# Distance attention of a decoder: both query halves in one group of products, value products between the groups

## The chip, the cores and the metric

The kernel runs on one core of a Trainium2 chip. The metric is the device time of one execution in microseconds (us), here the median of three runs.

## The reference, cut to what matters

The kernel is a two-layer decoder on x of 1024 tokens by 128 features. Six blocks follow one another, each with a residual sum and a layer norm. The change touches only the first, an attention whose weights come from distances, with 16 heads of width 64:

```python
P = X @ W_in + b_in                       # per head Q, K, V, G, 64 wide each
d2 = q2[..., :, None] + k2[..., None, :] - 2.0 * qk
cdist = jnp.sqrt(jnp.maximum(d2, 0.0))
W = jnp.power(EPS + cdist, -2)
W = W / (EPS + jnp.sum(W, axis=-1, keepdims=True))
A = jnp.einsum('hbts,hbse->hbte', W, V)
H = (G * A).transpose(1, 2, 0, 3).reshape(b, t, HEADS * 64)
return H @ W_out + b_out
```

q2 and k2 are the squared norms of the queries and of the keys. All of it is float32. The five blocks behind it (a gated network over a context of 6404 rows, two mixtures of experts, a rotary attention, a cross attention and a last attention) are the same in both kernels.

## The kernel before, in words

The stage is `distance_attention`. The order of work on each engine is written out by hand, and the engines meet in semaphores. The heads are taken as 8 pairs; the two heads of a pair stand in partitions 0 to 63 and 64 to 127. The stage goes through bodies b = 0 to 8 and a closing part. Body b makes the distances of pair b and, from b = 2 on, does the value products, sums and output of pair b - 2.

A body on TensorE, in this order: the projections to queries and keys (`project_qk`, line 193); from body 3 on the output projection of pair b - 3 (line 304); value products of key chunks 0 and 1 of pair b - 2 (line 240); the norms of the queries and of the keys (lines 201 and 206); the sums of the weights (line 250); value products of chunks 2 and 3; the projections to values and gates (lines 213 and 218); then for each of 8 chunks of 128 keys and each half of 512 queries the distances. One distance group is two products K*Q, one for each head, contracting 64 rows (line 224), and behind them two products that add the query norms, contracting 3 rows in bf16 (line 229: the norm is split in three bf16 parts that add up). In the chunks 0 to 3 the value products of chunks 4 to 7 stand ahead of the two groups.

PSUM (`PS`) has eight banks. Banks 0 to 3 are two slots of two banks each: everything that VectorE reads takes the slots in turn. `TURN` numbers what is made, `room` makes TensorE wait until VectorE has taken what stood in the slot before (`s_taken`), and `s_made` tells VectorE that a slot is full. Banks 4 and 5 add up the value products, banks 6 and 7 the output.

A body on VectorE: squares of the queries and keys (lines 354 to 362), the split of the query norms (lines 368 to 374, over 64 partitions), a copy of the key norms (line 377), the copy of the sums (line 385), bias on values and gates (lines 393 and 397), then for each chunk and half two instructions that add the key norm and cut at zero, from PSUM to the tile D (line 405), and last the gated product (line 415). ScalarE takes the root of four chunks at a time, then logarithm and exponential (lines 480 to 490). GpSimd adds the weights over chunks (lines 545 and 550).

Of the kernel before, what the change touches and what calls it, by code (L numbers as in the profile page):

```python
# [18 lines left out]
BF16 = mybir.dt.bfloat16  # L19
# [4 lines left out]
P = 128  # L24
T = 1024
HALF = 512
NT = T // P
# [5 lines left out]
PAIRS = HEADS // 2  # L33
D0 = 64
# [49 lines left out]
def half(ap, h):  # L84
    return ap[:, h * HALF:(h + 1) * HALF]


def distance_attention(nc, PS, x, w, Y, onesd, fixed):
# [4 lines left out]
    PIECE = NT // 2  # L93
    BODIES = PAIRS + 2
    LAST = PAIRS - 1

    def turns(b):

        made = ["q", "k", "q2", "k2"] if b < PAIRS else []
        dist = [("d", c, h) for c in range(NT) for h in range(2)] if b < PAIRS else []  # L100
        vg = ["v", "g"] if b < PAIRS else []
        return made + (["sum"] if b >= 2 else []) + (dist + vg if b == 0 else vg + dist)
# [10 lines left out]
    with ExitStack() as ctx:  # L113
        n = Names(nc, ctx, "dist")
# [1 line left out]
        wout = n.sb("wout", [P, PAIRS, P])  # L116
        bias = n.sb("bias", [P, 3, PAIRS])
        bv = n.sb("bv", [P, PAIRS * P])
        selq = n.sb("selq", [P, D0])
        selk = n.sb("selk", [P, 2])  # L120
        rows = n.sb("rows", [P, 2])
        Q = n.sb("Q", [P, T])
# [3 lines left out]
        G = n.sb("G", [P, 3, T])  # L126
        D = n.sb("D", [P, 2, 2, NT, T])
        k2 = n.sb("k2", [P, NT, 2])
        p0 = n.sb("p0", [D0, T], BF16)
        rest = sq[0:D0, 0, :]  # L130
        q2 = n.sb("q2", [D0, T], BF16)
        wsum = n.sb("wsum", [P, 2, T])
        ones = n.sb("ones", [P, D0])
        onesb = n.sb("onesb", [P, P], BF16)
# [28 lines left out]
        with nc.Block() as block:  # L163
# [17 lines left out]
            def _(pe):  # L181
                def room(b, k):

                    if TURN[b, k] >= 2:
                        pe.wait_ge(s_taken, TURN[b, k] - 1)
                    return slot(b, k)
# [7 lines left out]
                                             start=True, stop=True)  # L194
                        last.then_inc(s_made, 1)

                def norms(b):
                    at = room(b, "q2")
                    pe.wait_ge(s_sq, 2 * b + 1)
                    for h in range(2):  # L200
                        last = pe.matmul(PS[0:D0, at + h, :], selq[:, :], half(sq[:, 0, :], h), start=True, stop=True)
                    last.then_inc(s_made, 1)
                    at = room(b, "k2")
                    pe.wait_ge(s_sq, 2 * b + 2)
                    for c in range(NT):
                        last = pe.matmul(PS[:, at, 2 * c:2 * c + 2], sq[:, 1, c * P:(c + 1) * P], selk[:, :],
                                         start=True, stop=True, skip_group_check=True)
                    last.then_inc(s_made, 1)

                def project_vg(b):  # L210
                    at = room(b, "v")
# [6 lines left out]
                        last = pe.matmul(PS[:, at + h, :], wp[:, b % 2, 3 * P:4 * P], half(x, h), start=True, stop=True)  # L218
                    last.then_inc(s_made, 1)

                def distances(b, c, h):
                    at = room(b, ("d", c, h))
                    for s in range(2):
                        pe.matmul(PS[:, at + s, :], K[D0 * s:D0 * s + D0, c * P:(c + 1) * P],  # L224
                                  Q[D0 * s:D0 * s + D0, h * HALF:(h + 1) * HALF], start=True, stop=False)
                    if c == 0 and h == 0:
                        pe.wait_ge(s_q2, b + 1)
                    for s in range(2):
                        last = pe.matmul(PS[:, at + s, :], onesb[32 * s:32 * s + 3, :],  # L229
                                         q2[32 * s:32 * s + 3, h * HALF:(h + 1) * HALF], start=False, stop=True)  # L230
                    last.then_inc(s_made, 1)

                def values(p, c):

# [74 lines left out]
                for b in range(BODIES - 1):  # L309
                    if b < PAIRS:  # L310
                        project_qk(b)
                    if b == 0:
                        pe.wait_ge(s_const, 4 * 16)
                        pe.wait_ge(s_set, 4)
                    if b >= 3:
                        projection(b - 3)
                    if b >= 2:
                        values(b - 2, 0)
                        values(b - 2, 1)
                    if b < PAIRS:  # L320
                        norms(b)
                    if b >= 2:
                        sums(b - 2)
                    if b >= 2:
                        values(b - 2, 2)
                        values(b - 2, 3)
                    if 0 < b < PAIRS:
                        project_vg(b)
                    for c in range(NT):
                        if b >= 2 and c < PIECE:  # L330
                            values(b - 2, PIECE + c)
                        for h in range(2 if b < PAIRS else 0):
                            distances(b, c, h)
                    if b == 0:
                        project_vg(b)
                closing()
# [2 lines left out]
            def _(dve):  # L339
# [7 lines left out]
                def made(b, k):  # L347
                    dve.wait_ge(s_made, TURN[b, k] + 1)
                    return flat(PS[:, slot(b, k):slot(b, k) + 2, :])
# [13 lines left out]
                    dve.wait_ge(s_sq, 2 * b + 2)  # L363
                    dve.sem_inc(s_taken, 1)

                def norms(b):
                    of = made(b, "q2")[0:D0]
                    own.up(dve.tensor_copy(p0[:, :], of))
                    own.done()
                    dve.scalar_tensor_tensor(rest, p0[:, :], rows[0:D0, 0:1], of, ALU.mult, ALU.add).then_inc(s_taken, 1)  # L370
                    dve.wait_ge(s_taken, TURN[b, "q2"] + 1)
                    own.up(dve.tensor_copy(p0[:, :], rest))
                    own.done()
                    dve.scalar_tensor_tensor(q2[:, :], p0[:, :], rows[0:D0, 1:2], rest, ALU.mult, ALU.add
                                             ).then_inc(s_q2, 1)
                    of = made(b, "k2")
                    dve.tensor_copy(flat(k2), of[:, 0:2 * NT]).then_inc(s_taken, 1)
                    dve.wait_ge(s_taken, TURN[b, "k2"] + 1)

                def totals(p):  # L380

# [1990 lines left out]
def _layout(inputs):  # L2372

    f = {k: np.asarray(v) for k, v in inputs.items()}
    W = f["L0_attn_W_in"].reshape(P, PAIRS, 2, 4, D0)
    wpair = np.concatenate([W[:, :, h, i] for i in range(4) for h in range(2)], axis=2).transpose(1, 0, 2)
    b = f["L0_attn_b_in"].reshape(HEADS, 4, D0)
    selq = np.zeros((2, D0, 2, 32), np.float32)
    selk = np.zeros((2, D0, 2), np.float32)
    drows = np.zeros((4, 32, 2), np.float32)  # L2380
    for h in range(2):
        selq[h, :, h, 0:3] = 1.0
        selk[h, :, h] = -0.5
    drows[:, 1:3, 0] = drows[:, 2, 1] = -1.0
    a = {
        "xT": f["x"][0].T,
        "ident": np.eye(P, dtype=np.float32),
        "center": (np.eye(P) - 1.0 / P).astype(np.float32),
        "cols": _columns(f["L0_attn_b_out"], f["L1_xattn_bo"], f["L1_ffn_ln1_w"], f["L1_ffn_ln1_b"],
                         f["L1_ffn_ln2_w"], f["L1_ffn_ln2_b"]),  # L2390
        "wpair": wpair,
        "wout": f["L0_attn_W_out"].reshape(PAIRS, P, P).transpose(1, 0, 2),
        "dbias": b[:, (0, 1, 3)].reshape(PAIRS, 2, 3, D0).transpose(1, 3, 2, 0).reshape(P, 3, PAIRS),
        "selq": selq.reshape(P, D0),
        "selk": selk.reshape(P, 2),
        "drows": drows.reshape(P, 2),
        "bv": np.broadcast_to(b[:, 2].reshape(1, T), (P, T)),
        "ctx": _context(f["ctx_1024"][0]),
        "small0": _small(f["L0_ffn_router_W"], f["L0_ffn_router_b"], f["L0_ffn_b1"], f["L0_ffn_b2"]),
        "experts0": _experts(f["L0_ffn_W1"], f["L0_ffn_W2"]),  # L2400
        "small1": _small(f["L1_ffn_gate_w"], f["L1_ffn_gate_b"]),
        "experts1": _experts(f["L1_ffn_w1"], f["L1_ffn_w2"]),
        **_rotary(f["L1_attn_Wq"], f["L1_attn_Wk"], f["L1_attn_Wv"], f["L1_attn_Wo"]),
        **_aux(),
        **_cross(f["L1_xattn_Wk"], f["L1_xattn_Wv"], f["L1_xattn_Wq"], f["L1_xattn_Wo"]),
        "mask": f["mask_1x1xSxS2_ik1"][0, 0],
        "last_w": f["L1_ffn_w_qkv"],
        "last_wo4": f["L1_ffn_w_proj"].reshape(4, GROUPS, D8, P),
        "last_rows": np.zeros((P, 3, GROUPS), np.float32),
    }  # L2410
    wo4 = np.zeros((4, 32, GROUPS, P), np.float32)
    wo4[:, 0:D8] = a["last_wo4"].transpose(0, 2, 1, 3)
    a["last_wo4"] = wo4.reshape(P, GROUPS * P)
    for j in range(GROUPS):
        a["last_rows"][:, 0, j] = np.arange(P) // D8 % GROUPS == j
        a["last_rows"][:, 1, j] = np.arange(P) % 32 == D8 * ((j + 1) % GROUPS)
        a["last_rows"][:, 2, j] = np.arange(P) % 32 != D8 * ((j + 1) % GROUPS)
    return {k: np.ascontiguousarray(v) for k, v in a.items()}
# [13 lines left out]
```

## Time and profile before

| what | us |
|---|---|
| median of 3 runs | 2407.54 (2407.51 to 2410.68) |
| the profiled execution | 2405.06 |
| its span in the profile | 2403.4 |
| TensorE busy | 2235.0 (93%) |
| ScalarE busy | 1630.8 (68%) |
| VectorE busy | 950.3 (40%) |
| GpSimd busy | 476.3 (20%) |

The span is what the records cover; 1.7 us of the execution lie around it. The busy shares are means over stages with different limits, so they say little on one stage. The stage of the change takes about the first 468 us of the span, the other five blocks the rest.

### The profile page before, as it was taken

Reading aid. Unit: us, or ns where it says so; the run is one execution under the profiler, and the core shown is the slowest. Engines: PE = TensorE matmul, PEld = TensorE weight load, DVE = VectorE, ACT = ScalarE, POOL = GpSimd, SP = SyncE. Lnnn points to the kernel's source line nnn. Section 1 sums busy time; section 2 is a strip of 40 time slices with the busy share of each in tenths; the row PEclk is TensorE's granted clock in tenths of the full one; section 3 lists DMA queues with packets and bytes.
Section 4 is the critical chain, followed back from the end, with each engine's and each line's share of the span. In section 5 each row is a group of like instructions: output and inputs, shape, how many; then the busy total and the mean of one; then the engine's idle time right before and its main releaser. Section 6 shows DMA issues by size and latency. Waiting matters only on the chain. (4 is left out here: it accounts for less than half of the span.)

```text
span 2403.4 us, 30487 instructions
## 1 busy us (share of the span) xinstructions
PE 2235.0 (93%) x12206; PEld 769.8 (32%) x12206; DVE 950.3 (40%) x1489; ACT 1630.8 (68%) x1295; POOL 476.3 (20%) x254
## 2 busy tenths in 40 slices
PE   8999999899979988999899999999999987999898
PEld 3333333344446632222311111111111122222466
DVE  7766676235441156666211111111111115887111
ACT  4998889633333223555599999999999964666533
POOL 0776665200100024666300000000000000000000
PEclk8999999999989998999999999999999996999999
DMA  1000000036644002000100010010000000000010
GB/s 43 9 5 5 5 1 1 27 140 213 208 159 160 26 0 71 1 1 1 23 24 1 1 43 1 1 43 1 1 1 1 1 2 9 1 1 1 21 35 26
DMA packets 29133, 79.00 MB, mean 33 GB/s; under 512 B 3600, under 2 KB 18976, under 8 KB 26928
## 3 DMA queue, kind: packets, MB, share of 16 engines
q1 hardware_dynamic: 15032, 30.71, 4.1%
q0 software_dynamic: 4384, 29.56, 3.5%
q10 hardware_dynamic: 9592, 16.96, 1.9%
q8 instruction: 89, 1.46, 0.2%
q14 instruction: 36, 0.29, 0.0%
HBM read 71.68 MB, written 5.59 MB: 32 GB/s over the span
## 5 line engine op out<-in xcount | busy, mean ns | idle before, releaser
L1889 ACT ACTIVATE crat_E<-banks 128x1536 f32<-128x1536 f32 x536 | 741.7, 1460 | 22.1 <-PE banks L1780 6.8
L1805 PE MATMUL banks<-crat_E,crat_vst 128*32 128x512 f32 (+1 forms) x3264 | 436.3, 607 | 0.5 <-ACT crat_E L1889 0.4
L1780 PE MATMUL banks<-crat_Q,mid_arena 52*128 52x512 bf16 x1600 | 322.7, 385 | 19.5 <-ACT crat_E L1889 15.3
L1916 DVE COPY crat_vst<-all_crossV 128x96 f32<-128x96 f32 x136 | 34.3, 253 | 635.5 <-PE banks L1805 635.4
L550 POOL TENSOR_TENSOR dist_wsum<-dist_wsum,dist_D 128x1024 f32<-128x1024 f32 x88 | 208.1, 2364 | 7.8
L1509 ACT ACTIVATE rotat_E<-banks 128x1024 f32<-128x1024 f32 x128 | 124.0, 1021 | 116.1 <-PE banks L1393 116.0
L405 DVE TENSOR_SCALAR dist_D<-banks,dist_k 128x512 f32<-128x512 f32 x256 | 178.8, 746 | 54.7 <-PE banks L229 53.6
L1780 PEld LDWEIGHTS banks<-crat_Q,mid_arena 52*128 52x128 bf16 x1600 | 59.3, 93 | 435.3 <-ACT crat_E L1889 300.9
L1575 DVE TENSOR_REDUCE rotat_mx<-banks 128x1 f32<-128x512 f32 x256 | 163.5, 685 | 70.0 <-PE banks L1364 68.8
L1509 ACT ACTIVATE lastat_E<-banks 128x1024 f32<-128x1024 f32 x128 | 123.9, 1020 | 85.6 <-PE banks L1385 85.6
L1575 DVE TENSOR_REDUCE lastat_mx<-banks 128x1 f32<-128x512 f32 x256 | 162.4, 685 | 37.8 <-PE banks L1364 35.1
L1521 POOL MEMSET lastat_mb<- 128x2048 f32 x1 | 1.8, 1805 | 802.1 <-POOLq L63 802.1
L1557 POOL TENSOR_TENSOR mid_arena<-rotat_E 128x2048 f32<-128x2048 f32 x31 | 140.4, 4528 | 89.3 <-ACT rotat_E L1509 86.0
L224 PE MATMUL banks<-dist_Q,dist_K 64*128 64x512 f32 x512 | 148.1, 656 | 4.7 <-DVE dist_sq L370 0.5
L843 ACT ACTIVATE mlp_A<-banks 128x1024 f32<-128x1024 f32 x51 | 52.2, 1024 | 136.1 <-PE banks L736 136.1
L940 PEld LDWEIGHTS banks<-moe_W,moe_A 128*128 128x128 f32 x1024 | 122.9, 192 | 45.8 <-issue 26.5
L940 PE MATMUL banks<-moe_W,moe_A 128*128 128x128 f32 x1024 | 125.7, 276 | 11.1 <-DVE moe_acc L1042 11.1
L1805 PEld LDWEIGHTS banks<-crat_E,crat_vst 128*32 128x32 f32 (+1 forms) x3264 | 64.3, 108 | 175.3 <-issue 163.5
L1042 DVE SCALAR_TENSOR_TENSOR moe_acc<-banks,moe_G,moe_acc 128x128 f32<-128x128 f32 x128 | 34.6, 344 | 209.9 <-PE banks L940 209.9
L240 PE MATMUL banks<-dist_D,dist_V 128*64 128x512 f32 x480 | 111.7, 601 | 0.0
L736 PE MATMUL banks<-all_x,mlp_C 128*128 128x512 f32 x204 | 100.2, 616 | 10.1 <-DMA mlp_C<-in_ctx 10.1
L480 ACT ACTIVATE dist_D<-dist_D 128x4096 f32<-128x4096 f32 x24 | 85.5, 3610 | 33.9 <-DVE dist_D L405 33.9
(271 smaller groups left out, 2807.1 us busy)
## 6 DMA issues: line engine op xcount, KB each, us to landing
mlp_M<-in_mask POOLq DMA_DIRECT2D x28, 800.5 KB
mid_arena<-cross_k SPq DMA_DIRECT2D x42, 204.0 KB
moe_W<-in_experts SPq DMA_DIRECT2D x16, 512.0 KB, 3.6
mid_arena<-in_rot_tables ACTq DMA_DIRECT2D x8, 1024.0 KB, 19.2
mlp_C<-in_ctx SPq DMA_DIRECT2D x17, 384.0 KB, 4.5
cross_k<-mlp_kp ACTq DMA_DIRECT2D x17, 288.0 KB, 2.3
mlp_row<-in_mask POOLq DMA_DIRECT2D x1, 3202.0 KB, 12.7
mlp_M<-in_mask POOLq DMA_DIRECT2D x1, 3202.0 KB
```

The lines of the kernel that those rows point to most:

```text
L224: pe.matmul(PS[:, at + s, :], K[D0 * s:D0 * s + D0, c * P:(c + 1) * P], Q[D0 * s:D0 * s + D0, h * HALF:(h + 1) * HALF], start=True, stop=F ...
L240: last = pe.matmul(PS[D0 * s:D0 * s + D0, 4 + h, :], V[:, p % 3, c, D0 * s:D0 * s + D0], D[:, p % 2, s, c, h * HALF:(h + 1) * HALF], start ...
L405: last = dve.tensor_scalar(D[:, b % 2, s, c, h * HALF:(h + 1) * HALF], of[:, s * HALF:(s + 1) * HALF], k2[:, c, s:s + 1], 0.0, ALU.add, AL ...
L550: pool.tensor_tensor(to, to, W[:, c, :], ALU.add).then_inc(s_add, 1)
L736: last = pe.matmul(PS[:, at + h, :], C[:, b, k, 0:P], half(x, h), start=True, stop=True)
L940: last = pe.matmul(PS[:, Y[k] + t // 4, (t % 4) * P:(t % 4 + 1) * P], A[:, f % 2, t * P:(t + 1) * P], W[:, k, FF + f * P:FF + (f + 1) * P] ...
L1509: act.activation(flat(E[:, at % NE, 2 * i:2 * i + 2, :]), flat(PS[:, S + 2 * i:S + 2 * i + 2, :]), ACT.Exp, scale=scale).then_inc(s_e, 1)
L1557: pool.tensor_tensor(flat(ES[:, (4 * ps + k) % 2, :, :]), flat(E[:, at % NE, :, :]), flat(E[:, (at + 1) % NE, :, :]), ALU.add).then_inc(s_ ...
L1575: dve.tensor_reduce(mx[:, t, r, kh:kh + 1], PS[:, MX + i % 2, :], AX.X, ALU.max).then_inc(s_mt, 1)
L1780: last = pe.matmul(PS[:, 3 * (at % 2) + k, :], K[s:s + ROWS, 2 * (g % 2) + pair, c * P:(c + 1) * P], Q[s:s + ROWS, 2 * g + pair, qh * HALF ...
L1805: last = pe.matmul(PS[32 * j:32 * j + 32, 6 + ps % 2, :], vst[keys, (ps * STEPS + c // 3) % 3, c % 3, j, :], E[keys, at // 3 % NE, at % 3, ...
L1889: act.activation(flat(E[:, at % NE, :, :]), flat(PS[:, 3 * (at % 2):3 * (at % 2) + 3, :]), ACT.Exp, scale=CROSS_SCALE).then_inc(s_e, 1)
```

## The change

The two distance groups of a chunk become one: products K*Q of the first query half, then of the second, and behind all four the norm products of both halves. For this both slots have to be free before the group is complete. The query norms are now made in four groups of 32 partitions (so `selq` is 128 wide, and `p0`, `rest` and `q2` have 128 partitions), so that the four norm products contract different row groups. The value products of chunks 2 to 7 stand one behind each of the groups 0 to 5. From body 1 on the key norms are made ahead of the query norms.

```diff
+    def norm_order(b):
+        return ["q2", "k2"] if b == 0 else ["k2", "q2"]
-        made = ["q", "k", "q2", "k2"] if b < PAIRS else []
+        made = ["q", "k"] + norm_order(b) if b < PAIRS else []
-        selq = n.sb("selq", [P, D0])
+        selq = n.sb("selq", [P, P])
-        p0 = n.sb("p0", [D0, T], BF16)
-        rest = sq[0:D0, 0, :]
-        q2 = n.sb("q2", [D0, T], BF16)
+        p0 = n.sb("p0", [P, T], BF16)
+        rest = sq[:, 0, :]
+        q2 = n.sb("q2", [P, T], BF16)
...
-                def distances(b, c, h):
-                    at = room(b, ("d", c, h))
-                    for s in range(2):
-                        pe.matmul(PS[:, at + s, :], K[D0 * s:D0 * s + D0, c * P:(c + 1) * P],
-                                  Q[D0 * s:D0 * s + D0, h * HALF:(h + 1) * HALF], start=True, stop=False)
-                    if c == 0 and h == 0:
+                def distances(b, c):
+                    ats = []
+                    for h in range(2):
+                        ats.append(room(b, ("d", c, h)))
+                        for s in range(2):
+                            pe.matmul(PS[:, ats[h] + s, :], K[D0 * s:D0 * s + D0, c * P:(c + 1) * P],
+                                      Q[D0 * s:D0 * s + D0, h * HALF:(h + 1) * HALF], start=True, stop=False)
+                    if c == 0:
                         pe.wait_ge(s_q2, b + 1)
-                    for s in range(2):
-                        last = pe.matmul(PS[:, at + s, :], onesb[32 * s:32 * s + 3, :],
-                                         q2[32 * s:32 * s + 3, h * HALF:(h + 1) * HALF], start=False, stop=True)
-                    last.then_inc(s_made, 1)
+                    for h in range(2):
+                        for s in range(2):
+                            r = D0 * h + 32 * s
+                            last = pe.matmul(PS[:, ats[h] + s, :], onesb[r:r + 3, :], q2[r:r + 3, h * HALF:(h + 1) * HALF],
+                                             start=False, stop=True)
+                        last.then_inc(s_made, 1)
...
-                    if b >= 2:
-                        values(b - 2, 2)
-                        values(b - 2, 3)
                     if 0 < b < PAIRS:
                         project_vg(b)
                     for c in range(NT):
-                        if b >= 2 and c < PIECE:
-                            values(b - 2, PIECE + c)
-                        for h in range(2 if b < PAIRS else 0):
-                            distances(b, c, h)
+                        if b < PAIRS:
+                            distances(b, c)
+                        if b >= 2 and c + 2 < NT:
+                            values(b - 2, c + 2)
```

VectorE's `norms` is split in the same way into `query_norms` and `key_norms`, called in `norm_order`, and reads 128 partitions where it read 64.

## Rows read from the trace of the kernel before

**Rows 1.** The page: the span, and busy time of each engine.
```profile
span 2403.4 us, 30487 instructions
PE 2235.0 (93%) x12206; PEld 769.8 (32%) x12206; DVE 950.3 (40%) x1489; ACT 1630.8 (68%) x1295; POOL 476.3 (20%) x254
```

**Rows 2.** Busy time in body 3 (window, length, engines, granted clock, DMA).
```profile
140.07:194.53 54.46, 53.00 (x220) 18.37 (x221) 36.74 (x46) 47.34 (x16) 38.63 (x17) 0.97 0.02 5
```

**Rows 3.** TensorE in time (start, length, group), body 3, chunk 0.
```profile
165.78 1.13 PE L224 MATMUL banks<-dist_Q,dist_K 64*128 64x512 f32 x4
166.84 0.39 PE L229 MATMUL banks<-dist_q,dist_onesb 3*128 3x512 bf16 x2
167.16 1.13 PE L224 MATMUL banks<-dist_Q,dist_K 64*128 64x512 f32 x4
...
168.22 0.39 PE L229 MATMUL banks<-dist_q,dist_onesb 3*128 3x512 bf16 x2
...
168.54 1.94 PE L240 MATMUL banks<-dist_D,dist_V 128*64 128x512 f32 x8
```

**Rows 4.** TensorE and VectorE in time, body 3, chunks 4 to 6.
```profile
182.62 1.13 PE L224 MATMUL banks<-dist_Q,dist_K 64*128 64x512 f32 x4
183.68 0.39 PE L229 MATMUL banks<-dist_q,dist_onesb 3*128 3x512 bf16 x2
184.00 1.13 PE L224 MATMUL banks<-dist_Q,dist_K 64*128 64x512 f32 x4
184.11 2.79 DVE L405 TENSOR_SCALAR dist_D<-banks,dist_k 128x512 f32<-128x512 f32 x4 [0.17 <-PE banks L229]
185.57 1.13 PE L224 MATMUL banks<-dist_Q,dist_K 64*128 64x512 f32 x4
...
187.07 2.79 DVE L405 TENSOR_SCALAR dist_D<-banks,dist_k 128x512 f32<-128x512 f32 x4 [0.17 <-PE banks L229]
```

**Rows 5.** TensorE in time, from the last distances of body 2 on.
```profile
139.47 0.39 PE L229 MATMUL banks<-dist_q,dist_onesb 3*128 3x512 bf16 x2
140.07 3.67 PE L193 MATMUL banks<-all_x,dist_wp 128*128 128x512 f32 x8 [0.21 <-DVE dist_D L405]
...
150.69 1.95 PE L206 MATMUL banks<-dist_selk,dist_sq 128*128 128x2 f32 x16
153.37 3.47 PE L250 MATMUL banks<-dist_wsum,dist_ones 128*64 128x512 f32 x8 [0.74 <-DVE dist_sq L370]
```

**Rows 6.** VectorE in time, body 3, between projections and distances.
```profile
150.79 1.22 DVE L368 CAST dist_p<-banks 64x1024 bf16<-64x1024 f32 x1 [3.08 <-PE banks L201]
152.05 1.27 DVE L370 SCALAR_TENSOR_TENSOR dist_sq<-dist_p,dist_rows,banks 64x1024 f32<-64x1024 bf16 x1
155.28 0.16 DVE L377 COPY dist_k<-banks 128x16 f32<-128x16 f32 x1
164.02 1.28 DVE L397 TENSOR_SCALAR dist_G<-banks,dist_bias 128x1024 f32<-128x1024 f32 x1 [0.49 <-PE banks L218]
```

**Rows 7.** TensorE in time: the key norms of body 1.
```profile
56.12 2.27 PE L206 MATMUL banks<-dist_selk,dist_sq 128*128 128x2 f32 x16 [0.84 <-DVEq L364]
```

**Rows 8.** Busy time and granted clock (the number behind POOL) in four stretches.
```profile
24.00:26.00 2.00, 2.00 (x6) 0.60 (x6) 0.86 (x3) 0.00 (x0) 0.00 (x0) 0.50 0.00 0
54.00:56.00 2.00, 1.27 (x3) 0.14 (x1) 1.94 (x2) 2.00 (x2) 0.00 (x0) 1.00 0.00 0
58.00:60.00 2.00, 1.68 (x8) 1.60 (x9) 1.93 (x3) 2.00 (x2) 0.00 (x0) 0.50 0.00 0
153.30:156.70 3.40, 3.33 (x10) 1.02 (x12) 2.06 (x4) 3.40 (x2) 0.00 (x0) 0.53 0.00 0
```

**Rows 9.** ScalarE in time: the roots of the second half of pair 3.
```profile
195.80 7.12 ACT L480 ACTIVATE dist_D<-dist_D 128x4096 f32<-128x4096 f32 x2 [4.71 <-DVE dist_D L405]
```

**Rows 10.** TensorE in time behind the last distances of the stage.
```profile
415.26 3.17 PE L304 MATMUL banks<-dist_H,dist_wout 128*128 128x512 f32 x4 [2.64 <-DVE dist_H L415]
...
444.99 7.05 PE L258 MATMUL banks<-dist_D,dist_V 128*64 128x512 f32 x16
```

More of the change, by code:

```diff
@@ L195, in project_qk, with query_norms @@
                         last.then_inc(s_made, 1)
-                def norms(b):
+                def query_norms(b):
                     at = room(b, "q2")
@@ L200, in norms, with key_norms @@
                     for h in range(2):
-                        last = pe.matmul(PS[0:D0, at + h, :], selq[:, :], half(sq[:, 0, :], h), start=True, stop=True)
+                        last = pe.matmul(PS[:, at + h, :], selq[:, :], half(sq[:, 0, :], h), start=True, stop=True)
                     last.then_inc(s_made, 1)
+                def key_norms(b):
                     at = room(b, "k2")
@@ L208, in norms @@
                     last.then_inc(s_made, 1)
+                def norms(b):
+                    for k in norm_order(b):
+                        if k == "q2":
+                            query_norms(b)
+                        else:
+                            key_norms(b)
                 def project_vg(b):
@@ L364, in squares, with query_norms @@
                     dve.sem_inc(s_taken, 1)
-                def norms(b):
-                    of = made(b, "q2")[0:D0]
+                def query_norms(b):
+                    of = made(b, "q2")
                     own.up(dve.tensor_copy(p0[:, :], of))
                     own.done()
-                    dve.scalar_tensor_tensor(rest, p0[:, :], rows[0:D0, 0:1], of, ALU.mult, ALU.add).then_inc(s_taken, 1)
+                    dve.scalar_tensor_tensor(rest, p0[:, :], rows[:, 0:1], of, ALU.mult, ALU.add).then_inc(s_taken, 1)
                     dve.wait_ge(s_taken, TURN[b, "q2"] + 1)
@@ L373, in norms, with key_norms @@
                     own.done()
-                    dve.scalar_tensor_tensor(q2[:, :], p0[:, :], rows[0:D0, 1:2], rest, ALU.mult, ALU.add
-                                             ).then_inc(s_q2, 1)
+                    dve.scalar_tensor_tensor(q2[:, :], p0[:, :], rows[:, 1:2], rest, ALU.mult, ALU.add).then_inc(s_q2, 1)
+                def key_norms(b):
                     of = made(b, "k2")
@@ L378, in norms @@
                     dve.wait_ge(s_taken, TURN[b, "k2"] + 1)
+                def norms(b):
+                    for k in norm_order(b):
+                        if k == "q2":
+                            query_norms(b)
+                        else:
+                            key_norms(b)
                 def totals(p):
@@ L2377, in _layout @@
     b = f["L0_attn_b_in"].reshape(HEADS, 4, D0)
-    selq = np.zeros((2, D0, 2, 32), np.float32)
+    selq = np.zeros((2, D0, 2, 2, 32), np.float32)
     selk = np.zeros((2, D0, 2), np.float32)
@@ L2381, in _layout @@
     for h in range(2):
-        selq[h, :, h, 0:3] = 1.0
+        selq[h, :, :, h, 0:3] = 1.0
         selk[h, :, h] = -0.5
@@ L2393, in _layout @@
         "dbias": b[:, (0, 1, 3)].reshape(PAIRS, 2, 3, D0).transpose(1, 3, 2, 0).reshape(P, 3, PAIRS),
-        "selq": selq.reshape(P, D0),
+        "selq": selq.reshape(P, P),
         "selk": selk.reshape(P, 2),
```

## The prediction

> **What bounds the kernel now.** I read the page first: TensorE is busy for 93% of the span, no other engine for more than 68% [rows 1]. The change touches only the first stage, so I cut that by bodies. Body 3 takes 54.46 us, TensorE is busy for 53.00 of it, ScalarE for 47.34, VectorE for 36.74 [rows 2]. TensorE looks like the bound. But the rows in time show two kinds of chunk. In chunks 0 to 3 a group of distances costs 1.38 us (165.78 to 167.16: 1.06 for four K*Q instructions, 0.32 for the norm products) and the value products ahead of the groups 1.87, so a chunk takes 2 x 1.38 + 1.87 = 4.63 [rows 3]. In chunks 4 to 7 there are no value products, and a chunk should take 2.76; it takes 2.95 (182.62 to 185.57) [rows 4]. That is the slots. TensorE fills a slot in 1.06 + 0.39, VectorE starts 0.04 later and reads it in 2.79 / 2 = 1.40, TensorE starts again 0.06 later: 1.45 + 0.04 + 1.40 + 0.06 = 2.95. While VectorE reads one slot, TensorE fills the other; VectorE rests only 0.17 between two chunks [rows 4]. What the reader should keep: here it is the hand-over of slots that counts, not only TensorE's work.
>
> **The merged group, part by part.** TensorE's work falls. A chunk has one change from K*Q to norm products instead of two, and four norm products side by side. The work becomes 1.06 + 0.86 + 0.32 = 2.24 instead of 2.76, where 0.86 is what four K*Q instructions take without the change behind them; I read it as half of the 1.87 less the start, eight instructions of the same 512 columns (0.43 for a pair) [rows 3]. If the second pair of norm products doesn't run beside the first, it adds 0.32 per chunk to the work, but VectorE then still starts on the first half as early; what is late is at most 0.1 us. I take nothing.
>
> The hand-over gets worse. The norm products of the first half now stand behind the K*Q products of the second, and those wait for the second slot. VectorE gets both halves at once, reads both, and gets the next chunk only after the second slot was freed, refilled and finished. From the start N of the norm products: 0.43 to VectorE's start, 2.79 for both halves, 0.06, then 1.06 for the K*Q products of the second half: 4.34 to the next norm products [rows 4]. The K*Q products of the first half lie in VectorE's reading time, and so do value products behind the group: 0.32 + 1.87 = 2.19, first half until 3.05, before 3.28. So a chunk takes 4.34 with or without value products. Nothing in the rows makes it shorter; at the low clock it is longer (below).
>
> Distances of bodies 2 to 7: seven steps between the norm products of chunk 0 (second half) and chunk 7 take 3 x 4.63 + 4 x 2.95 = 25.7 now and 7 x 4.34 = 30.4 after, +4.7 each, six times: +28.2. Bodies 0 and 1 have no value products: 7 x (4.34 - 2.95) = +9.7 each; body 0 started at the low clock [rows 8] with steps that were longer already, so +9.0 there. Together +18.7.
>
> **Ahead of the distances.** Value products 2 and 3 move away from here (-3.5, into time that TensorE now waits), and key norms go first. From 139.47 to 168.22, last norm products to last of chunk 0, body 3 needs 28.75 us [rows 3, 5]. After, counted from N: the query projection waits until the first half is read (0.43 + 1.40 + 0.06 = 1.89; now it starts at 0.60). Then queries and keys 3.6 to 5.5, output projection 1.8, value products 0 and 1 3.65 (two groups of 1.94 less their overlap), key norms 1.8, query norms 1.8: 14.6. The sums follow at once, since the slot of the key norms is freed by a copy of 0.16 [rows 6]: the wait of 0.74 goes [rows 5], and they take 1.8 if the clock is up (3.47 now, where it was 0.53 [rows 5, 8]): 16.4. The value projection waits for the second instruction of the norm split, 1.22 + 1.27 behind the query norms: 17.2, ends 19.1. The gate projection waits for the copy of the sums, behind the rest of the split (the whole takes 4.49, 150.79 to 155.28 [rows 6]) and 1.2 of copy: starts 20.5, ends 22.35. VectorE adds its bias in 1.28 [rows 6] and only then are K*Q products of the second half possible: 23.8 + 1.06 = 24.9. So -3.85 in each of bodies 3 to 7, -19.3. Body 2 has no output projection and no low clock now: 23.1 against 25.4 (28.75 less 1.8 and 1.5), -2.3. Splitting over 128 instead of 64 partitions I cost at nothing: the bias instruction over 128 partitions takes as long (1.28) as the split's 1.27 over 64 [rows 6]. The selector is twice as large (32 KB more of loading); it is used behind the first squares, which cover it; uncovered it is well below 1 us.
>
> Body 1 has nothing between projections and norms. Key norms wait for the squares of the keys [rows 7] and the query norms follow 1.9 later, where they now stand first. That and the later projections (1.6) I put at +3.6.
>
> **The end.** Behind the last distances TensorE waits 2.64 for the gated product [rows 10]; VectorE reaches it a half later, +1.4. ScalarE is no bound: it waits 4.71 for the second half of a pair [rows 9], and its 47.34 fit in a body of 55.
>
> Sum at the full clock: 28.2 + 18.7 - 19.3 - 2.3 + 3.6 + 1.4 = +30.3 us.
>
> **The clock.** The clock is at 0.50 of its speed, 1.2 instead of 2.4 GHz, from 58 us on, after a stretch in which TensorE was busy 1.27 of 2.00 us, and at 24 to 26 us it was still low although TensorE was busy all the time with distances; around the sums it falls after the nearly empty key norms [rows 8]. After the change TensorE works 2.24 of 4.34 us in bodies 0 and 1, a half. I expect the clock to be low for much of them. At the low clock a step is TensorE's: first half possible at 0.65 + 1.40 + 0.06 = 2.11, K*Q 1.7, then 2.0: 5.8 (twice the rows' 0.86 and 1.06). Between 4.34 and 5.8 I take 5.3, nearer the low rows because distances alone didn't lift it at 24 us. That is 15 steps x 0.95 = +14. In bodies 2 to 6 groups 6 and 7 have no value products behind them and TensorE then waits for the first slot; one fall there costs what it costs at the sums now, 3.47 - 1.94 = 1.5 [rows 3, 5], five times: +7.5. With both: +52, from 0 (no fall) to about +37 above the 30.3 (low through bodies 0 and 1, 15 x 1.5 = 22, and twice 7.5).
>
> The Trainium skill, TensorE: Matmul & The Clock Gate, Part 1, says that the throttled state is the default and activity releases it. The rows agree in kind: the clock stood at 0.50 behind 1.27 of 2.00 us [rows 8]. By that rule the waits that the change adds are paid twice.
>
> **Rivals.** (a) The waits stay short enough for the full clock: +30, 2438 us. For it: at 54 to 56 us the clock was still full with a third of the time empty [rows 8]. (b) The clock is low throughout the first two bodies and longer at each turn: +67, 2474. (c) The other side: TensorE's work is what counts, the slots cost nothing. Then 64 chunks save 0.52 (-33), the 0.19 by which 32 chunks miss 2.76 goes (-6), and the low clock at the sums goes in five bodies (-7.5): -47, 2361. It decides if VectorE can start on the first half before the second slot is refilled. TensorE busy 53.00 of 54.46 [rows 2] speaks for it; the order of the products in the diff speaks against it, and the 2.95 instead of 2.76 [rows 4] shows that slots bind even now. (d) The four norm products disturb each other (+0.3 a chunk on the path): +20 on top of (a) or 2478 on top of the forecast; the two of now don't.
>
> The Trainium skill, TensorEngine Tiling (Array Packing), Key Properties, says that a change of tiling mode drains the array. The row agrees: 1.06 for four K*Q instructions before the norm products against 0.86. By that rule alone the change wins, as in (c).
>
> **How the numbers follow.** The profiled execution took 2405.06, 2.5 below the median of 2407.54; 1.7 lie around its span, untouched. I add the difference to the median. Forecast 2407.5 + 52 = 2459, chance 0.53; (a) 0.24; (b) 0.10; (c) 0.05; (d) 0.04; 0.04 for small effects in between. The range from 2432 to 2478 leaves out (c) and the far part of (b) and (d). Less than 0.2% (4.8 us) can't be told from no change. Faster 0.05, same 0.02, slower 0.93.
>
> **What would show it.** VectorE's four instructions of a chunk (line 405) begin 4.3 to 5.8 us apart in every chunk of every body, with 1.5 us or more of waiting for the norm products, where it is 0.17 now; TensorE's K*Q products wait for line 405 in each chunk; bodies 3 to 7 take 55 to 57 us; the clock in bodies 0 and 1 is well below 1. The prediction is wrong if chunks 6 and 7 take 3 us, or if TensorE's waits for VectorE are gone.

## The result and the profile after

The changed kernel takes 2472.59 us (median of 4 runs, 2466.09 to 2473.66) against 2409.11 (2407.51 to 2411.96): 1.0257 times the time, 95% interval 1.0235 to 1.0278. The prediction said 2459, range 2432 to 2478, slower with 0.93.

The profiled execution of the changed kernel took 2471.79 us. Its page, the lines that answer to [rows 1]:

```profile
span 2470.1 us, 30492 instructions
PE 2247.4 (91%) x12206; PEld 776.5 (31%) x12206; DVE 948.4 (38%) x1489; ACT 1630.9 (66%) x1295; POOL 477.3 (19%) x254
```

The span grew by 66.7. TensorE's busy time grew by only 12, though the change takes work from it: what grew is waiting, and instructions at the low clock. TensorE in time, end of body 3 (it answers to [rows 3, 4]):

```profile
234.69 1.94 PE L257 MATMUL banks<-dist_D,dist_V 128*64 128x512 f32 x8
236.56 2.15 PE L239 MATMUL banks<-dist_Q,dist_K 64*128 64x512 f32 x8
238.64 0.39 PE L246 MATMUL banks<-dist_q,dist_onesb 3*128 3x512 bf16 x4
240.54 1.13 PE L239 MATMUL banks<-dist_Q,dist_K 64*128 64x512 f32 x4 [1.50 <-DVE dist_D L427]
241.85 1.13 PE L239 MATMUL banks<-dist_Q,dist_K 64*128 64x512 f32 x4 [0.19 <-DVE dist_D L427]
242.92 0.39 PE L246 MATMUL banks<-dist_q,dist_onesb 3*128 3x512 bf16 x4
244.90 5.37 PE L197 MATMUL banks<-all_x,dist_wp 128*128 128x512 f32 x8 [1.59 <-DVE dist_D L427]
```

VectorE in the same stretch (each row is one chunk):

```profile
234.80 2.73 DVE L427 TENSOR_SCALAR dist_D<-banks,dist_k 128x512 f32<-128x512 f32 x4 [1.55 <-PE banks L246]
239.07 2.73 DVE L427 TENSOR_SCALAR dist_D<-banks,dist_k 128x512 f32<-128x512 f32 x4 [1.55 <-PE banks L246]
243.35 2.73 DVE L427 TENSOR_SCALAR dist_D<-banks,dist_k 128x512 f32<-128x512 f32 x4 [1.55 <-PE banks L246]
```

The last step, 238.64 to 242.92, has no value products before its K*Q products; the one before it, 234.37 to 238.64, has them. Both take 4.28 us: 2.73 of reading and 1.55 in which VectorE waits for the norm products. In [rows 4] the wait was 0.17 and the step 2.95. The last row of TensorE shows the price behind it: the projections of the next body take 5.37 instead of 3.67 [rows 5], with a granted clock of 0.67 from 244.9 to 250.0 us.

In the other bodies with value products the last step is not always 4.28. It is in bodies 3 and 5; in bodies 2, 4, 6 and 7 it takes 5.33 to 5.51, because the clock has fallen already (0.53 from 410.0 to 413.6). The end of body 6:

```profile
408.07 0.40 PE L246 MATMUL banks<-dist_q,dist_onesb 3*128 3x512 bf16 x4
409.97 3.68 PE L239 MATMUL banks<-dist_Q,dist_K 64*128 64x512 f32 x8 [1.50 <-DVE dist_D L427]
413.58 0.39 PE L246 MATMUL banks<-dist_q,dist_onesb 3*128 3x512 bf16 x4
```

Body 0 of the changed kernel, TensorE:

```profile
45.52 3.79 PE L239 MATMUL banks<-dist_Q,dist_K 64*128 64x512 f32 x8 [1.50 <-DVE dist_D L427]
49.24 0.61 PE L246 MATMUL banks<-dist_q,dist_onesb 3*128 3x512 bf16 x4
51.35 3.78 PE L239 MATMUL banks<-dist_Q,dist_K 64*128 64x512 f32 x8 [1.50 <-DVE dist_D L427]
55.06 0.39 PE L246 MATMUL banks<-dist_q,dist_onesb 3*128 3x512 bf16 x4
```

The step from 49.24 to 55.06 is 5.82. The seven steps of body 0 take 5.10 to 5.84, 5.5 on the mean. Busy time and granted clock (the number behind POOL) from 17 to 45 and 45 to 90 us of the changed kernel:

```profile
17.00:45.00 28.00, 19.89 (x60) 5.42 (x60) 14.50 (x22) 8.62 (x5) 0.00 (x0) 0.63 0.00 1
45.00:90.00 45.00, 32.21 (x106) 16.39 (x108) 26.41 (x28) 30.20 (x12) 10.21 (x4) 0.73 0.04 12
```

and of the kernel before:

```profile
17.00:45.00 28.00, 26.73 (x97) 7.16 (x96) 23.45 (x34) 12.41 (x7) 0.00 (x0) 0.82 0.00 1
45.00:90.00 45.00, 42.18 (x169) 18.16 (x168) 38.52 (x48) 41.94 (x14) 26.51 (x12) 0.92 0.04 12
```

Where the difference arises, by start times of the norm products in the two profiled executions, in us:

| stretch | predicted | measured |
|---|---|---|
| start and distances of body 0 | +16 | +15.4 |
| from there to the first group of body 1 | +3.6 | +9.8 |
| distances of body 1 | +17 | +17.8 |
| ahead of the distances, bodies 2 to 7, low clock included | -14 | -13.8 |
| distances of bodies 2 to 7 | +28 | +29.9 |
| end of the stage | +1.4 | +2.5 |
| other stages | 0 | +5.0 |

The first product of the next stage starts 61.7 us later, at 540.78 instead of 479.10 (the first row is of the kernel before, the second of the changed one):

```profile
479.10 6.21 PE L736 MATMUL banks<-all_x,mlp_C 128*128 128x512 f32 x8 [5.05 <-DMA mlp_C<-in_ctx]
```
```profile
540.78 6.55 PE L758 MATMUL banks<-all_x,mlp_C 128*128 128x512 f32 x8 [4.99 <-DMA mlp_C<-in_ctx]
```

The rest up to 66.7 comes in the five blocks behind it, whose code is the same. It is not the change's doing as far as the traces tell: from this product to the end of the span, five of the twelve traces of this case take 1923.6 to 1924.7 us (the kernel before, e1, e2, e4, e7) and seven take 1927.9 to 1929.3 (the changed kernel, e3, e5, e6, e8, e9, and also e10, which has the order of the kernel before). What sets the two lengths apart is open.

### The profile page after: what moved, and what is told of

Same layout as the page of the kernel before. It is cut to its first block and busy times, and to the rows that moved or that the text cites. A ratio compares the mean times of both kernels' runs of the same rounds, so it can differ in the third digit from the quotient of the medians.

```text
span 2470.1 us, 30492 instructions
## 1 busy us (share of the span) xinstructions
PE 2247.4 (91%) x12206; PEld 776.5 (31%) x12206; DVE 948.4 (38%) x1489; ACT 1630.9 (66%) x1295; POOL 477.3 (19%) x254
## 5 line engine op out<-in xcount | busy, mean ns | idle before, releaser
L239 PE MATMUL banks<-dist_Q,dist_K 64*128 64x512 f32 x512 | 166.0, 757 | 37.7 <-DVE dist_D L427 31.6
```

The lines of the kernel that those rows point to most:

```text
L239: pe.matmul(PS[:, ats[h] + s, :], K[D0 * s:D0 * s + D0, c * P:(c + 1) * P], Q[D0 * s:D0 * s + D0, h * HALF:(h + 1) * HALF], start=True, st ...
```

## The experiments

The kernel before, run beside them, took 2409.35, 2411.29 and 2409.56 us (medians of three sets of runs; each ratio below is to the set run beside it).

**e1: the halves as two groups again.** Of the changed kernel only this is different:

```diff
-                    ats = []
                     for h in range(2):
-                        ats.append(room(b, ("d", c, h)))
+                        at = room(b, ("d", c, h))
...
-                    for h in range(2):
                         for s in range(2):
...
```

(the norm products of a half follow its own K*Q products).

> The changed kernel with the two query halves as two distance groups again, each finished before the next begins; value products behind chunks 0 to 5, key norms first and norms in four row groups stay. If merging the halves is what costs: chunks without value products take 2.95 us again, chunks with them 2 x 1.38 + 1.87 = 4.63, VectorE waits 0.17 in the former, and the time is about 2416 us (+7 over the kernel before: key norms first costs body 1 about 5, value products behind the later chunks some 2). If the new places of value products and norms cost instead, it stays near 2472.

2416.03 us (2414.95 to 2420.14), ratio to the kernel before 1.0034 (1.0020 to 1.0049). Undoing the merge alone gives back 57 of 63 us, as expected (2416). VectorE, body 2, chunks 6 and 7:

```profile
147.09 2.79 DVE L425 TENSOR_SCALAR dist_D<-banks,dist_k 128x512 f32<-128x512 f32 x4 [1.84 <-PE banks L244]
150.04 2.79 DVE L425 TENSOR_SCALAR dist_D<-banks,dist_k 128x512 f32<-128x512 f32 x4 [0.17 <-PE banks L244]
```

With value products ahead of it a chunk waits 1.84, without them 0.17: 4.63 and 2.95 us, as before the change.

What is left is mostly in body 1: from the last norm products of body 0 to the last ones of chunk 0 of body 1 e1 takes 28.97 us, against 22.85 in the kernel before and 32.68 in the changed one.

**e2: only the merge** (with the four row groups of the norms that it needs), all other work where it stood in the kernel before.

```diff
-    return ["q2", "k2"] if b == 0 else ["k2", "q2"]
+    return ["q2", "k2"]
+                    if b >= 2:
+                        values(b - 2, 2)
+                        values(b - 2, 3)
...
+                        if b >= 2 and c < PIECE:
+                            values(b - 2, PIECE + c)
                         if b < PAIRS:
                             distances(b, c)
-                        if b >= 2 and c + 2 < NT:
-                            values(b - 2, c + 2)
```

> The kernel before with nothing but the merged group (and the four row groups that it needs); value products and norms stand where they stood. If merging costs: every chunk step is 4.28 us at the full clock and about 5.5 in bodies 0 and 1, with value products ahead of a group hidden in it, and the time is about 2480 us, a little over the changed kernel, since value products 2 and 3 are then not hidden. If the places cost: near 2409.

2508.01 us (2506.83 to 2510.01), 1.0409 (1.0392 to 1.0426): the merge alone costs 99 us, more than the whole change. My 2480 was too low by 28: I took 4.28 for chunks 4 to 7 of the later bodies, but in four chunks in a row without value products the clock is low there too. The steps of chunks 4 to 7 are 4.79 to 5.84, and the distances of bodies 2 to 7 take 27.5 us more than at 4.28 a step. Busy time and clock of e2 around such a stretch:

```profile
230.00:257.00 27.00, 19.21 (x68) 5.06 (x62) 14.49 (x23) 8.13 (x3) 15.96 (x7) 0.69 0.00 0
```

So the spread of the value products and the order of the norms, which the change made together with the merge, hide 35 us of the merge's cost.

**e3: work added to keep TensorE busy.** In bodies 0 and 1 products that nobody reads stand behind each group:

```diff
+                        if b < 2:
+                            for h in range(2):
+                                for s in range(2):
+                                    pe.matmul(PS[D0 * s:D0 * s + D0, 4 + h, :], x[:, c * P + D0 * s:c * P + D0 * s + D0],
+                                              half(x, h), start=True, stop=True, skip_group_check=True)
```

> The changed kernel with products added that nobody reads, behind each distance group of bodies 0 and 1, of the size of the value products (banks 4 and 5, not in use there). 64 instructions for each half more work. If the low clock is paid because TensorE waits half the time: the granted clock in these bodies rises to 1.0 after the first chunks, steps go from 5.5 to 4.28 us, and the time falls by about 16 us to 2456 although work is added. If the clock is low for another reason, or if TensorE's work binds: no change, or slower by up to 16 x 1.87 = 30 us (2502).

2451.21 us (2448.24 to 2455.19): 21 less than the changed kernel, with 30 us of TensorE work more (16 times 1.87). TensorE in body 0 of e3, and its first window:

```profile
36.58 2.15 PE L239 MATMUL banks<-dist_Q,dist_K 64*128 64x512 f32 x8
38.66 0.39 PE L246 MATMUL banks<-dist_q,dist_onesb 3*128 3x512 bf16 x4
38.99 1.94 PE L351 MATMUL banks<-all_x 128*64 128x512 f32 x8
40.85 2.15 PE L239 MATMUL banks<-dist_Q,dist_K 64*128 64x512 f32 x8
42.94 0.40 PE L246 MATMUL banks<-dist_q,dist_onesb 3*128 3x512 bf16 x4
```
```profile
17.00:45.00 28.00, 27.16 (x120) 7.33 (x120) 17.80 (x27) 8.70 (x5) 0.00 (x0) 0.94 0.00 1
```

The step is 4.28 (38.66 to 42.94), the clock 0.94 instead of 0.63. The added products lie wholly in the wait. The step doesn't go below 4.28: that part is the hand-over. In the traces the distances of bodies 0 and 1 take 16.7 us less than in the changed kernel (30.00 and 30.66 against 38.79 and 38.53), about what was expected. The rest of the gain is not in the two bodies: chunk 7 is slow in one of bodies 2 to 7 instead of four, though the edit doesn't touch them.

**e5: three slots.**

```diff
-            return 2 * (TURN[b, k] % 2)
+            return (0, 2, 6)[TURN[b, k] % 3]
-                    if TURN[b, k] >= 2:
-                        pe.wait_ge(s_taken, TURN[b, k] - 1)
+                    if TURN[b, k] >= 3:
+                        pe.wait_ge(s_taken, TURN[b, k] - 2)
...
-                    for h in range(2):
-                        of = pe.matmul(PS[:, Y + h, :], wout[:, p, :], half(H, h), start=(p == 0), stop=(p == LAST),
...
+                    pe.sem_inc(s_proj, 1)
```

> The changed kernel with three slots (banks 6 and 7 as the third) instead of two. To free these banks the output projections of pairs 0 to 6 are left out, 1.8 us of TensorE in each of six bodies; the result then lacks them. If the hand-over of slots makes the 4.28 us step: a chunk without value products takes 2.8 to 3.0 us, VectorE waits at most 0.2 between chunks, chunks with value products take TensorE's 4.1 to 4.3, the clock in bodies 0 and 1 stays up, and the time is near 2395 us. If what makes the step is something in the merged group itself (the norm products of four row groups, the change of mode): the steps stay at 4.28 and 5.5, and the time is about 2460 (only the projections gone).

2396.16 us (2 runs, 2394.86 and 2397.46). End of body 2, TensorE:

```profile
136.62 0.40 PE L246 MATMUL banks<-dist_q,dist_onesb 3*128 3x512 bf16 x4
136.94 1.13 PE L239 MATMUL banks<-dist_Q,dist_K 64*128 64x512 f32 x4
138.51 1.13 PE L239 MATMUL banks<-dist_Q,dist_K 64*128 64x512 f32 x4 [0.44 <-DVE dist_D L424]
139.57 0.40 PE L246 MATMUL banks<-dist_q,dist_onesb 3*128 3x512 bf16 x4
```

With the same merged group, a third slot gives 2.95 instead of 4.28. The group costs nothing by itself; its need of both slots does. Chunks with value products take 4.11 us: that is TensorE's own work, the 2.24 of the prediction and 1.87 of value products, 0.52 less than the 4.63 of the kernel before. The clock does better than in the changed kernel, but isn't full: 0.94 from 17 to 45 us and 0.85 from 45 to 90. About 13 of the 76 us are the projections left out (seven of 1.8).

**e4: key norms first, halves apart,** value products where they stood before. **e10** is the same with the query norms first everywhere, so the wider norms alone.

```diff
+    def norm_order(b):
+        return ["q2", "k2"] if b < 2 else ["k2", "q2"]
```

> The kernel before (two groups per chunk, value products where they stood, norms in four row groups) with the key norms ahead of the query norms from body 2 on. If the wait of the sums for VectorE (0.74) and the low clock behind the key norms (1.5) both come from that order: 2.2 us less in each of bodies 3 to 7 and 0.7 in body 2, 2397 us. If the clock falls as before: 4 less, 2405. If the later query norms hold the first distances back: no gain, 2409.

> The kernel before with nothing but the query norms made in four row groups (selector 128 wide, split over 128 partitions, the norm products of the second half from partitions 64 and 96); the order of everything stays. If that part of the change costs nothing: 2409 us, same. If the wider split or weights cost: the split instructions are longer than 1.27 and 0.69, or the norm products of a half than 0.39, and the time grows by 8 times that, 2 to 5 us.

e4: 2393.60 us (2392.54 to 2397.78), ratio 0.9939 (0.9922 to 0.9955), 0.6% less than the kernel before and clear of the noise; 2397 was expected. TensorE in body 3 of e4 (it answers to [rows 5]):

```profile
150.11 1.96 PE L205 MATMUL banks<-dist_sq,dist_selq 128*128 128x512 f32 x4
152.00 1.94 PE L265 MATMUL banks<-dist_wsum,dist_ones 128*64 128x512 f32 x8
```

The sums follow without the 0.74 and take 1.94 instead of 3.47. Body 3 takes 52.23 (139.40 to 191.63) instead of 54.46. e10: 2408.61 us (2404.59 to 2418.26), ratio 0.9997 (0.9983 to 1.0012). The wider norms cost nothing that can be seen; the split instructions take 1.284 and 0.694 us instead of 1.276 and 0.686.

**e6: query norms first in body 1 too. e9: GpSimd's first addition held back.** Both are the changed kernel otherwise.

```diff
-    return ["q2", "k2"] if b == 0 else ["k2", "q2"]
+    return ["q2", "k2"] if b < 2 else ["k2", "q2"]
```
```diff
+                    if p == 0 and s == 0:
+                        pool.wait_ge(s_q2, 2)
```

> The changed kernel with the query norms ahead of the key norms in body 1 as well (key norms first only from body 2). The stretch of body 1 from the last distances of body 0 to its own first ones took 32.7 us against 22.9 before. If the order does that (TensorE idle for 3.8 us ahead of the norms, and the split of the query norms so late that it runs beside GpSimd's additions, one instruction 3.26 us instead of 1.28): VectorE's last split instruction is back at 1.28, the stretch falls to about 26, 6 us less, 2466 us. If it is the low clock alone that stretches it: 1 or 2 us less.

> The changed kernel with GpSimd's first addition held back until VectorE has finished the split of the query norms of body 1 (one wait on a semaphore that counts these splits). In the changed kernel the last split instruction of body 1 runs beside GpSimd's additions and takes 3.26 us, in the other bodies 1.28. If the two disturb each other: it takes 1.28 us again, the first distances of body 1 come about 2.3 us sooner (32.7 becomes 30.4), and the time is 2470 us or so; GpSimd's own lateness of some 6 us is covered, since it waits for ScalarE later. If the length has another reason (the low clock, the data): it stays at 3.26 and the time at 2472.

VectorE and GpSimd in body 1 of the changed kernel:

```profile
81.92 2.37 POOL L572 TENSOR_TENSOR dist_wsum<-dist_wsum,dist_D 128x1024 f32<-128x1024 f32 x1
84.36 2.68 POOL L572 TENSOR_TENSOR dist_wsum<-dist_wsum,dist_D 128x1024 f32<-128x1024 f32 x1
87.19 3.17 POOL L572 TENSOR_TENSOR dist_wsum<-dist_wsum,dist_D 128x1024 f32<-128x1024 f32 x1
...
83.84 0.99 DVE L386 CAST dist_p<-dist_sq 128x1024 bf16<-128x1024 f32 x1
84.87 3.26 DVE L388 SCALAR_TENSOR_TENSOR dist_q<-dist_p,dist_rows,dist_sq 128x1024 bf16<-128x1024 bf16 x1
```

and of e9:

```profile
83.65 0.69 DVE L386 CAST dist_p<-dist_sq 128x1024 bf16<-128x1024 f32 x1
84.37 1.28 DVE L388 SCALAR_TENSOR_TENSOR dist_q<-dist_p,dist_rows,dist_sq 128x1024 bf16<-128x1024 bf16 x1
...
85.81 2.37 POOL L569 TENSOR_TENSOR dist_wsum<-dist_D 128x1024 f32<-128x1024 f32 x1 [85.23 <-DVE dist_q L388]
```

With GpSimd away, 3.26 is 1.28 and 0.99 is 0.69: it was the overlap. GpSimd pays too: its additions take 2.68 and 3.17 us beside VectorE's instructions instead of 2.37. The stretch of body 1 fell from 32.7 to 29.1 us, 3.6 where 2.3 were expected, but in the time of the whole it doesn't stand out: 2467.73 (2460.50 to 2469.24), ratio 1.0241 (1.0227 to 1.0255) against 1.0257 (1.0235 to 1.0278). e6 took 2457.56 us (2453.69 to 2461.45). The order in body 1 is worth more than the 6 I gave it: the stretch fell to 27.35, 5.3 less, and the distances of body 1 took 2.0 less at a better clock. But my reason was half wrong: the split instruction still ran beside GpSimd and took 3.50. What e6 gained is TensorE's idle time, not the overlap. Of its 15 us 7.3 lie there. Another 4.1 lie in bodies 6 and 7, which the edit doesn't touch: the clock does not fall at their ends in this trace, so chunk 7 takes 4.28 instead of 5.51 and 5.46, and the stretch between the two bodies 25.03 instead of 26.73. The rest is 1.3 at the end of the stage and 1.4 in the later blocks.

**e7 and e8: a version that beats both.** e7 is e4 with the merged group only where value products stand behind it; e8 adds to e7 products that nobody reads around the norms of bodies 0 and 1 (8 in body 0, 6 in body 1, where I had written 6 in each; `fill(2)` is four products of 64 by 512, each contracting 128 rows).

```diff
+                        if b < PAIRS:
+                            if b >= 2 and c < PIECE:
+                                merged(b, c)
+                            else:
+                                distances(b, c)
+                        if b >= 2 and c < PIECE:
+                            values(b - 2, PIECE + c)
```
```diff
+                    if b < 2:
+                        fill(2)
                     if b < PAIRS:
                         norms(b)
+                    if b < 2:
+                        fill(2 - b)
```

> The kernel with key norms first from body 2 (2393.6), and the merged group only in chunks 0 to 3 of bodies from 2 on, where the value products of chunks 4 to 7 stand behind it; the other chunks have two groups. By the steps measured, 4.28 with value products merged against 4.63 apart: about 1.2 us less in each of six bodies, 2386 us. If the passage from merged to separate groups costs a wait of the slot: 2394, no gain.

> The same with products that nobody reads in TensorE's waits around the norms of bodies 0 and 1 (6 products of 128 by 512 in body 0 and 1 each at most, banks 4 and 5). If the low clock at the start (from 16.6 to 26.8 us and 57.5 to 64.4 in the kernel before) follows from these waits: it is gone, 5 us less, 2381. If the clock is low whatever stands there: the same as without, or 1 us more for the added work.

e7: 2390.75 us (2385.25 to 2392.54), ratio 0.9913 (0.9899 to 0.9926). Body 3 takes 51.05 (136.44 to 187.49), 1.18 less than in e4, as expected. In the time of the whole this isn't shown: I expected 2386, the median is 2.9 us below that of e4, and the intervals of the two ratios overlap. e8: 2383.27 (2381.92 to 2385.42), ratio 0.9879 (0.9863 to 0.9894), against the kernel before at 2411.29. Its windows:

```profile
17.00:45.00 28.00, 26.92 (x122) 8.88 (x119) 25.40 (x37) 13.77 (x8) 0.00 (x0) 1.00 0.00 1
45.00:90.00 45.00, 44.39 (x181) 16.10 (x181) 40.79 (x49) 44.94 (x16) 29.44 (x13) 1.00 0.04 12
```

The clock is full throughout, where it was 0.88 and 0.96 in e7 and 0.82 and 0.92 in the kernel before. The intervals of e7 and e8 don't overlap, and by medians the products save 7 us (5 were expected). The traces show 3.6 of them in the stage: the next one starts at 455.31 instead of 458.86. The two profiled executions took the same time (2385.25 and 2385.42), since behind the stage that of e8 is one of the longer ones.

## Why the prediction was right, point by point

- **The sum.** +52 predicted, +63.5 by the medians, +66.7 in the profiled executions; the range held it. Of the 14.7 us missing in the profile 6.2 lie in body 1, 5.0 in the later blocks, 1.9 in the distances of bodies 2 to 7 and 1.1 at the end of the stage.
- **The hand-over: right, shown.** 4.34 predicted, 4.28 measured with and without value products where the clock is full. e1 takes it away by the order, e5 by a third slot. The second pair of norm products costs nothing, as I took it: four take 0.39 us as two did.
- **The clock: right in kind, a little small.** 5.3 for a step in bodies 0 and 1, 5.54 and 5.50 measured, 0.2 too little 14 times. e3 shows that the low clock is a second price of the waits: 16.7 us come back in these bodies when TensorE has work in them, though nobody reads it. In bodies 2 to 7 the sum came out close partly by luck. At 4.28 a step the full clock gives +25.3, not +28.2. The falls of the clock cost about 11 instead of the 7.5 I gave them: 4.6 at chunk 7 in four bodies, where I had none, 1.7 each ahead of the distances of bodies 4, 6 and 7, and about as much in body 2.
- **Ahead of the distances: right.** With the value products moved and the key norms first it is 25.0 to 25.2 us at the full clock from the last norm products to the next (24.9 predicted), 26.7 where the clock fell at the turn. In body 2 it is 25.5 where I had 23.1, with its first projections at the low clock (5.35 us). Bodies 3 to 6 take 54.9 us where the clock stays up and 57.8 to 57.9 where it falls; I had said 55 to 57. The wait of 0.74 and the 3.47 are gone.
- **Body 1: the step that was mis-sized.** "That and the later projections (1.6) I put at +3.6": measured +9.8. The later projections are 1.8. The rest of my sum had the query norms 1.9 us later, but they start 10.1 us behind the query projection instead of 4.7: the key norms wait for the squares of the keys, TensorE stands still for 3.8 us instead of 1.1, and only then come the key norms and the query norms. Two things more were missing: the value projection ran at the low clock from body 0 (3.48 us instead of 2.05), and the split met GpSimd's additions (1.98 + 0.30 us more). e1 shows how much of it is the order of the norms without the merge: 6.1 of the 9.8. The full clock alone does not help here: in e3 the value projection takes 2.05, but the split meets GpSimd for longer (2.21 and 3.25 us), and the stretch is 32.65 as before.
- **"Splitting over 128 instead of 64 partitions I cost at nothing": right** (e10), but the split was also moved later, and there I named no cover. The Trainium skill, SBUF — State Buffer, section "SBUF: two separate sides", says that a VectorE instruction with two SBUF inputs and a GpSimd instruction that reads SBUF exclude each other for the whole instruction. The rows agree: the split begins at 84.87, GpSimd's addition of 84.36 ends at 87.04, and the split ends at 88.13; the next addition, begun at 87.19, takes 3.17 us instead of 2.37. So 3.26 is 1.98 of waiting and 1.28 of work, and e9 takes the waiting away. That page would have corrected my sum, had I drawn POOL's start beside the moved instruction.
- **The end: +2.5 for +1.4.** The wait for the gated product is 1.3 longer (3.95 us), and behind it the granted clock is 0.50 (475.7 to 479.4), where it was 0.61 (415.2 to 418.4).
- **Rival (c), TensorE's work as the bound: wrong with two slots.** The 0.52 that a merged group saves is there: with a third slot a chunk with value products takes 4.11 instead of 4.63 (e5). With two slots 0.35 of it is left in such chunks (4.28, e7), and the others lose 1.33.
- **Open:** executions of the changed kernel differ by 7.6 us (2466.09 to 2473.66) and of e9 by 8.7. The traces show two things of this size that differ without an edit in that place: the bodies at whose end the clock falls (up to 1.2 us at chunk 7 and 1.7 behind it), and the two lengths of the later blocks, some 4 us apart. What decides either is not shown.

## What to carry to other kernels

Before merging two groups that share a pair of buffers, write down the loop from the reader's start to its next start: with both buffers needed at once, reading and refilling no longer overlap, whatever work was saved. Merge only where other work lies in that wait. A wait of TensorE can cost twice: look at the granted clock of each stretch where the change adds waits, and at what runs on the neighbouring engines where it moves an instruction.

## What the runs showed of the hardware that I had not expected

- Work added to TensorE can make a kernel faster: 30 us more of products, 21 us less time (e3); 14 more products in the first two bodies take the clock from 0.88 and 0.96 to 1.00 (e8 against e7).
- In the kernel before, the records have TensorE busy all of 17.54 to 26.70 us and the granted clock was 0.50 throughout; it was 1.00 from 27 us on, with the same kind of work going on. In the changed kernel and in e3 it rose at 21 us already. In the changed kernel, where TensorE then waited, it was back at 0.52 from 24 to 31 us; in e3, with products in the waits, it was 0.99 from 21 to 30 us and 1.00 from 30 to 58.
- An instruction of VectorE from two tiles in SBUF took 3.25 to 3.50 us instead of 1.28 beside GpSimd's additions, in every kernel where the two met (the changed one, e1, e3, e5, e6), while the reading of PSUM beside the same additions kept its 2.73 a chunk. The cast ahead of it took 0.99 to 2.21 us instead of 0.69 in three of these kernels (the changed one, e3, e5).
